# Decoder megakernel on one core: values ahead of keys, router steps moved between slots, masks added strip by strip

## The reference, cut to what matters

```python
# layer 0: keys and values from ctx, queries from x, keys masked; then a dense feed-forward part
scores = jnp.where(mask == 0, -1e20, einsum('bqhd,bkhd->bhqk', q, k))
x = layernorm(softmax(scores / sqrt(256)) @ v @ w_out + b_out + query, g1, beta1)
x = layernorm(relu(x @ w_ff1 + b_ff1) @ w_ff2 + b_ff2 + x, g2, beta2)
# layer 1: cross attention with ctx, residual, layernorm
# layer 2: self attention with a causal mask
scores = jnp.where(tril(ones(S, S)), scores, -inf)
# layer 3: cross attention with ctx, then the experts
router_weights = softmax(x @ rw + rb); topw, topi = top_k(router_weights, 2)
out = sum of the two chosen experts' gelu feed-forward outputs, weighted by softmax(topw)
# layer 4: attention with ctx, one key and value head, keys within 64 of the query; gate, RMS norm
keep = (j >= i - 64) & (j < i + 65)
scores = jnp.where(keep, scores, -1e9)
```

## Time and profile before

| what | value |
|---|---|
| median of 3 runs | 2574.62 us (2570.72 to 2575.63) |
| the profiled execution: its time, its span | 2572.03 us, 2570.2 us |
| busy, share of the span: PE, DVE, ACT, POOL | 90%, 59%, 42%, 37% |
| mean granted clock of TensorE | 0.975 of full speed |

### The profile page before, as it was taken

How to read it: one execution, slowest core, us unless ns; L and a number is a source line. 1 busy time by engine, 2 the same in 40 slices (tenths; PEclk the granted TensorE clock), 3 DMA queues, 4 the chain that set the end, 5 groups by cost and what they waited for, 6 DMA issues and landing times. The chain is left out here.

```text
span 2570.2 us, 78594 instructions
## 1 busy us (share of the span) xinstructions
PE 2325.6 (90%) x29652; PEld 1900.8 (74%) x29653; DVE 1525.4 (59%) x3344; ACT 1079.6 (42%) x2772; POOL 944.7 (37%) x1190
## 2 busy tenths in 40 slices
PE   6999899899899899899898994999999997999997
PEld 4867767767767767767766864999999994666665
DVE  4676676676677677677676676111111114888885
ACT  2344334334334334334334342555555552444443
POOL 3434354344344354354344353200000004556662
PEclk9999999999999999999999997999999997999998
DMA  9201001001001001000000002511111111111110
GB/s 214 95 2 35 2 18 31 6 18 31 5 19 31 6 19 31 6 18 31 6 18 19 2 19 88 173 37 37 35 36 37 37 33 52 50 55 51 51 55 19
DMA packets 89114, 98.12 MB, mean 38 GB/s; under 512 B 23808, under 2 KB 80288, under 8 KB 88736
## 3 DMA queue, kind: packets, MB, share of 16 engines
q1 hardware_dynamic: 79040, 67.20, 8.7%
q0 software_dynamic: 9440, 27.29, 3.4%
q10 hardware_dynamic: 384, 0.01, 0.0%
HBM read 62.21 MB, written 32.24 MB: 37 GB/s over the span
## 5 line engine op out<-in xcount | busy, mean ns | idle before, releaser
L1365 DVE TENSOR_REDUCE mb<-ps_scores 128x8 bf16<-128x1024 f32 x320 | 377.5, 1220 | 107.9 <-PE ps_scores L767 107.8
L1727 POOL TENSOR_TENSOR qbd_all<-qT,consts 128x512 fp32r<-128x512 f32 x160 | 166.4, 1040 | 662.4 <-ACT kT L1112 264.0
L1374 DVE RECIPROCAL rs<-ps_o 128x256 f32<-128x256 f32 x160 | 280.8, 1755 | 43.8 <-PE ps_o L822 41.5
L1126 ACT ACTIVATE pt_all<-ps_scores 128x512 f32<-128x512 f32 x512 | 264.1, 604 | 71.6 <-PE ps_scores L795 71.6
L974 PEld LDWEIGHTS ps_scores<-tiles,w_now 128*128 128x128 f32 x2272 | 266.3, 193 | 5.7 <-ACT w_now L1197 1.3
L974 PE MATMUL ps_scores<-tiles,w_now 128*128 128x128 f32 x2272 | 266.9, 276 | 1.5 <-ACT w_now L1197 0.9
L984 PE MATMUL ps_w<-arena,tiles 128*128 x1136 | 257.1, 379 | 2.5 <-ACT tiles L1205 2.5
L1205 ACT ACTIVATE tiles<-ps_scores,b1s 128x128 f32<-128x128 f32 x568 | 154.1, 382 | 233.6 <-PE ps_w L984 231.2
L1833 POOL DMA_INDIRECT arena<-sorted_y,pidx x64 | 65.9, 1029 | 493.8 <-ACT pidx L1231 478.6
L984 PEld LDWEIGHTS ps_w<-arena,tiles 128*128 128x128 f32 x1136 | 210.4, 190 | 28.5 <-issue 2.9
L1750 POOL TENSOR_TENSOR rstd<-ve,neghalf 128x1 f32<-128x1 f32 x192 | 106.2, 553 | 338.2 <-DVE ve L1385 329.8
(11 more groups left out here) (237 smaller groups left out, 4844.8 us busy)
## 6 DMA issues: line engine op xcount, KB each, us to landing
tiles<-sorted_x SPq DMA_DIRECT2D x72, 128.0 KB, 2.0
sorted_y<-tiles SPq DMA_DIRECT2D x71, 128.0 KB, 1.7
w_experts<-in_L_xattn_e_w SPq DMA_DIRECT2D x6, 1024.0 KB, 12.3
arena<-in_L_xattn_e_w POOLq DMA_DIRECT2D x12, 384.0 KB, 4.1
ct_scratch<-cT SPq DMA_DIRECT2D x32, 128.0 KB, 1.7
x_scratch<-x2b_all SPq DMA_DIRECT2D x32, 128.0 KB, 1.7
arena<-x_scratch SPq DMA_DIRECT2D x32, 128.0 KB, 2.0
cT<-ct_scratch SPq DMA_DIRECT2D x32, 128.0 KB, 2.1
```

What stands on the lines that cost most here:

```text
L1126: nc.scalar.activation(pt[:, 4 * g:4 * g + 4, :].rearrange("p h q -> p (h q)"), ps_s[:, g, :], ACT.Exp, bias=bias, scale=LAYER[l]["scale"] ...
L1365: last = V.tensor_reduce(mb[:].rearrange("p (g r) -> p g r", g=BANKS)[:, 2 * half:2 * half + 2, 0:SLOTS], ps_s[:, 2 * half:2 * half + 2, : ...
L1374: V.reciprocal(rs[:], ps_o[:, 2:4, :]).then_inc(recip_ready, 1)
L1727: G.tensor_tensor(qbd[p].bitcast(F32R), qT[:].unsqueeze(2).to_broadcast([P, KC, PAIR, P]), hmask.unsqueeze(1).unsqueeze(3).to_broadcast([P ...
```

## The change: what it does

It does six things. (1) In light slots `project` makes values, then keys and queries, and waits for `mt_sb` only behind the values; in FF slots and in stage C (argument `keys_first`) layers 1, 3 and 4 make the keys first, as before. (2) Masks are added by strips of 32 rows: the causal and the window mask are stored as four blocks repeated in every strip, and each bank takes four matmuls of 32 rows and 128 columns in place of one of 128 rows and 512 columns; the key mask takes one matmul of 32 rows and 512 columns for each bank. (3) In slots 3 to 6 `router_pieces` stands last on VectorE, behind `qk_lo` and `relu_b`. (4) `rank`, `ranks`, `router_weights` and `positions` move from slot 7 to slot 6, where `rank` stands between `av` and `scores_t`, the scatters from slots 8 to 11 to 7 to 10; the tail of stage A is a slot shorter. (5) In slot 6 `scores_t(now)` stands ahead of `xt(nxt)`. (6) The masks are loaded later: 512 KB for the causal one behind layer 1's weights (waited for and converted on VectorE in slot 3 of iteration 0), 256 KB for the window between stages B and C, in place of 128 KB at the start. The key mask's row is loaded into all 128 partitions, and GpSimd's `mask_row` works on all of them.

```diff
@@ constants()
-    c[:, C_CAUSAL:C_WIN] = np.where(j <= i, 0.0, NEG)
-    c[:, C_WIN:C_ALL] = np.where((j >= i - WINDOW_HALF) & (j < i + WINDOW_HALF + 1), 0.0, NEG)
+    causal = np.where(j <= i, 0.0, NEG)
+    window = np.where((j >= i - WINDOW_HALF) & (j < i + WINDOW_HALF + 1), 0.0, NEG)
+    for at_, m in ((C_CAUSAL, causal.T), (C_CAUSAL + BANKS * P, causal), (C_WIN, window)):
+        blocks = m.reshape(BANKS, ROWS, P).transpose(1, 0, 2).reshape(ROWS, BANKS * P)
+        c[:, at_:at_ + BANKS * P] = np.tile(blocks, (BANKS, 1))
@@ SyncE
-        sp.dma_start(pt[:, 0:2, :], a["consts"][:, C_CAUSAL:C_ALL].rearrange("p (a b) -> p a b", a=2)).then_inc(ld_const, 16)
-            sp.dma_start(kmi[st][0:1, :], a["mask"][bass.ds(b, 1)]).then_inc(mask_loaded[st], 16)
+            sp.dma_start(kmi[st], a["mask"][bass.ds(b, 1)].rearrange("o k -> (o k)").partition_broadcast(P)).then_inc(mask_loaded[st], 16)
+                sp.dma_start(causal_f, a["consts"][:, C_CAUSAL:C_WIN]).then_inc(ld_causal, 16)
...
+        sp.wait_ge(b_down, TILES)
+        sp.dma_start(win_f, a["consts"][:, C_WIN:C_ALL]).then_inc(ld_window, 16)
@@ TensorE: project(n, first_l, keys_first)
-            wait(pe, mt_sb, t)
...
-            if l in (1, 3, 4):
+            keys_first = keys_first and l in (1, 3, 4)
+            if keys_first:
+                wait(pe, mt_sb, t)
                 keys()
             wait(pe, xt_sb, t + 1)
...
             last.then_inc(v_psum, 1)
+            wait(pe, mt_sb, t)
...
-                if l == 2:
+                if not keys_first:
                     keys()
@@
-        def masked(n, g, w, x_):
-            mm(ps_s[:, g, :].rearrange("p (h k) -> p h k", h=SLOTS), w, x_.unsqueeze(1).to_broadcast([P, SLOTS, P]),
-               start=True, stop=False)
+        def masked(blocks, strips):
+            for k in range(BANKS):
+                for g in strips:
+                    at_strip = slice(ROWS * g, ROWS * (g + 1))
+                    mm(ps_s[:, g, :].rearrange("p (h b k) -> p h b k", h=SLOTS, b=BANKS)[:, :, k, :], blocks[at_strip, k, :],
+                       ident_b[at_strip, ROWS * g:ROWS * (g + 1)].unsqueeze(1).to_broadcast([ROWS, SLOTS, ROWS]),
+                       start=k == 0, stop=False, tile_position=(ROWS * g, 0))
+        def keys_masked(n, strips):
+            for g in strips:
+                at_strip = slice(ROWS * g, ROWS * (g + 1))
+                mm(ps_s[:, g, :].rearrange("p (h k) -> p h k", h=SLOTS), ecol_b[at_strip, 0:1].to_broadcast([ROWS, P]),
+                   kmask[n["s"]][at_strip, :].unsqueeze(1).to_broadcast([ROWS, SLOTS, P]), start=True, stop=False,
+                   tile_position=(ROWS * g, 0))
@@ TensorE: run
-            ranked = routed(at_, 8)
+            ranked = routed(at_, 7)
...
-            if ranked:
+            if ranked and not ff_behind:
                 rank(ranked, ff["t"] if ff["ok"] else NT - 1)
...
                 av(prev)
+                if ranked:
+                    wait(pe, ffln_step, 5 * (rk_["j"] * NS + rk_["s"]) + 1)
+                    rank(ranked, ff["t"])
                 if ff["l"] == 0:
                     fxt(ff, 2)
-                    scores_t(now)
+                scores_t(now)
                 xt(nxt)
-                if ff["l"] != 0:
-                    scores_t(now)
-                project(nxt, first and nxt["s"] == 0)
+                project(nxt, first and nxt["s"] == 0, True)
@@ VectorE: run
+            if first and tau == 3:
+                dve.wait_ge(ld_causal, 16)
+                V.tensor_copy(causal_b.rearrange("p a b k -> p (a b k)"), causal_f).then_inc(causal_ready, 1)
...
-            if ranked:
+            if ranked and not (rk_["ok"] and rk_["l"] == 0):
                 ranks(ranked)
...
                 normalise(prev)
+                if ranked:
+                    ranks(ranked)
                 vz_evac(nxt)
-                router_pieces()
                 residual_sum()
                 qk_lo(nxt)
...
-                router_pieces()
             if ff["ok"] and ff["l"] == 0:
                 relu_b(ff)
+            router_pieces()
@@ VectorE, ahead of stage C
+        dve.wait_ge(ld_window, 16)
+        V.tensor_copy(win_b.rearrange("p b k -> p (b k)"), win_f).then_inc(window_ready, 1)
@@ GpSimd
-            G.tensor_scalar(kmask[n["s"]][0:1, :], kmi[n["s"]][0:1, :], 0.0, NEG, ALU.is_equal, ALU.mult).then_inc(kmask_ready, 1)
+            G.tensor_scalar(kmask[n["s"]], kmi[n["s"]], 0.0, NEG, ALU.is_equal, ALU.mult).then_inc(kmask_ready, 1)
...
-                if routed(at_, 9 + s):
-                    scatter(routed(at_, 9 + s), s)
+                if routed(at_, 8 + s):
+                    scatter(routed(at_, 8 + s), s)
```

More of the change, by code:

```diff
@@ L395, in program @@
         dict(scale=0.25, mask=None, bq=None, bk=None, bv=None),
-        dict(scale=0.25, mask=causal_b, bq="L2_xattn_sa_bq", bk="L2_xattn_sa_bk", bv="L2_xattn_sa_bv"),
+        dict(scale=0.25, mask="causal", bq="L2_xattn_sa_bq", bk="L2_xattn_sa_bk", bv="L2_xattn_sa_bv"),
         dict(scale=0.25, mask=None, bq="L2_xattn_ca_bq", bk="L2_xattn_ca_bk", bv="L2_xattn_ca_bv"),
-        dict(scale=0.25, mask=win_b, bq="L3_xattn_bq", bk=None, bv=None),
+        dict(scale=0.25, mask="window", bq="L3_xattn_bq", bk=None, bv=None),
     ]
@@ L752, in scores @@
                 wait(pe, kmask_ready, n["j"] * NS + n["s"] + 1)
+            if l == 2 and n.get("first_l"):
+                pe.wait_ge(causal_ready, 1)
             for half in range(2):
@@ L755, in scores @@
                 strips = range(2 * half, 2 * half + 2)
-                for g in strips:
-                    if mask == "keys":
-                        masked(n, g, one_b[:].to_broadcast([P, P]), kmask[n["s"]])
-                    elif mask is not None:
-                        masked(n, g, ident_b[:], mask[:])
+                if mask == "keys":
+                    keys_masked(n, strips)
+                elif mask is not None:
+                    masked(win_b if mask == "window" else causal_b[:, 0], strips)
                 for u in range(SLOTS):
@@ L779, in scores_t @@
             if not plain:
-                for g in range(BANKS):
-                    masked(n, g, mask[:], ident_b[:])
+                masked(win_b if mask == "window" else causal_b[:, 1], range(BANKS))
             first = plain
@@ L910, in run @@
             if first and tau == 0:
-                pe.wait_ge(ld_const, 32)
+                pe.wait_ge(ld_const, 16)
                 pe.wait_ge(consts_ready, 1)
                 xt(now)
-                project(now, True)
+                project(now, True, False)
+            now["first_l"] = first and now["s"] == 0
             if now["ok"]:
@@ L944, in run @@
                 if nxt["ok"]:
-                    project(nxt, first and nxt["s"] == 0 and nxt["l"] > 0)
+                    project(nxt, first and nxt["s"] == 0 and nxt["l"] > 0, False)
                 if now["ok"]:
@@ L1049, in run_c @@
                 pe.wait_ge(b_y, TILES)
+                pe.wait_ge(window_ready, 1)
                 xt(now)
[L1051 removed]
+                project(now, False, True)
             if now["ok"]:
@@ L1303, in _ @@
             V.memset(vz[i][:], 0.0)
-        for s in range(NS):
-            V.memset(kmask[s], 0.0)
         V.memset(onz[:, 0, 1, :], 0.0)
```

28 lines of the change are left out of this document (15 added, 13 removed).

## The result

The changed kernel takes 2477.04 us (median of 4 runs, 2471.51 to 2478.32) against 2572.67 us for the kernel before in the same comparison: a ratio of 0.9623, 95% interval 0.9604 to 0.9642. The profiled execution took 2476.19 us. The forecast was 2456, the range 2428 to 2500: the direction and the range held, and about 20 us of the expected gain did not come.

What follows compares the result with a forecast made beforehand. TensorE, busy 90% of the span, was taken as the bound, with VectorE nearly the bound in stage C. Terms of 46 + 38 + 16 + 16 = 116 us off 2572.0 gave 2456, range 2428 to 2500.

Steps and rivals of the forecast that it cites:

- Part 1: Light slots of stage A: values fill TensorE's wait for the copied maxima, 0.48 us a slot, 46 us (34 to 54).
- nothing late comes next: Light slots: queries still end the projection and everything behind the values moves up together, so 0.48 us a slot counts.
- Part 2: Stage A: masks by strips shorten TensorE's score matmuls, 4.8 us an iteration, 38 us in all (20 to 51).
- The masks are hardly cheaper: Rival, chance 0.12: new mask matmuls in stages A and C cost twice as much, giving 25 us in place of 54: 2485.
- Part 4: Stage A routing, 7 iterations: moved router steps gain 10.0 us, pay back 5.8 and 2.5; 16 us (-5 to 33).
- the two readings: Router's pieces at their new place on VectorE: 3.4 us by one profile reading, 2.7 by the rule with GpSimd idle.
- the slow clock eats the gain: Rival, chance 0.20: waits in slots 5, 6 and 7 bring 1.2 GHz stretches costing 4.2 us an iteration, not 2.5: 2472.
- Part 3: Stage C: masks by strips save 0.5 us in each of 32 slots, 16 us (9 to 19).
- The step that failed: Stage C: VectorE's waits of 0.28 and 0.25 us can give 0.53; 0.5 taken for each of 32 slots.
- what would show it: Signs: stage C slots of 11.9 to 12.0 us expected; one still above 12.3 would be wrong.
- Costed at nothing: Later mask loads, broadcast key mask, causal conversion on VectorE (once, about 1 us) and moved scatters: no cost counted.

Runs made afterwards that it cites:

- e1: The kernel before with only values made ahead of the wait for the copied maxima in light slots, masks and routing as before; ratio to before 0.9749.
- e2: The changed kernel with the routing move undone: router's pieces ahead of residual sum and `qk_lo`, rank and scatters one slot later; ratio to the kernel before 0.9710.
- e4: The changed kernel with stage C's expansion of the query remainders moved from GpSimd to ScalarE; ratio to the kernel before 0.9551, again 0.9501 (2448.23 us).
- e3: The changed kernel with stage C's window mask added as before, by matmuls of 128 rows and 512 columns; ratio to the kernel before 0.9648.
- e6: The changed kernel with the window masks of stage C (layer 4) left out; ratio to the kernel before 0.9635.
- e10: e9 with rank behind the product with the values in slot 9, ranks behind the reciprocal, weights in slot 8; 2425.80 us, ratio to the kernel before 0.9421.
- e8: The changed kernel with the router's pieces in smaller portions in slots 4 to 7, ranks, weights and positions in slot 8; ratio to the kernel before 0.9675.
- e7: The changed kernel with stage C's window mask as before and the query remainders expanded on ScalarE instead of GpSimd; ratio to the kernel before 0.9655.
- e9: The changed kernel with e4's move and e8's portions, but rank, ranks, weights and positions in slot 9; ratio to the kernel before 0.9494.

## Why the prediction was right, and where it was wrong

**Part 1 (46 us).** Right: 50 by e1, worked out from its iteration 0. The step that said nothing late comes next held; the gain was 0.52 a slot where 0.48 was taken.

**Part 2 (38 us).** Near, but less well shown: 35 by difference (106 less e1's 50 and e2's 21), from groups of both kinds, while e2 against e1, in one slower group, gives 8. By single stretches the masks' cost was read rightly. The second scores gave 0.75 (0.6 taken), the second half of the first 0.32 (0.3), slot 3 gave 0.63 (16.04 to 15.41 in iteration 0; 0.9 taken), slot 0 0.9 (8.9 in e1, 8.0 after; 0.1 taken), slot 1 0.1 (9.19 to 9.08). What the part left out is slot 2: 13.55 in e1, as much after where the clock stays up, and 15.1 to 15.2 in four of six iterations, some 6 us lost in all. *The masks are hardly cheaper* is out.

**Part 4 (16 us).** Right in sum, 21 by e2. By slots, before against after, slot 4 gained 1.6, slot 5 lost 0.2, slot 6 lost 1.6, slots 7 and 8 gained 5.0, of which 2.4 come in iteration 0 too and are not the routing's: 2.4 together, near the 2.3 forecast. The pieces took 3.1 us in the new place (441.89 to 445.01), between the 3.4 and the 2.7 of the two readings; two of them still last 0.45 and 0.51 in place of 0.19. Iterations 1 to 7 have 10 slow stretches, where the kernel before has 14. Six of the ten are in slot 7, behind the longest wait (2.44 us), four in slot 2, away from the router's steps, and none follow the waits of 1.05 and 1.69. So behind the late maxima there are 0.9 an iteration where 1.8 were taken, and *the slow clock eats the gain* did not happen.

**Part 3 (16 us).** Wrong, and it is the whole miss: -6 in place of +16. The step that failed is "VectorE's two waits (0.28 and 0.25) leave it 0.53 us to give. I take 0.5 for each of 32 slots". The waits did go (0.69 to 0.11 a slot), but the step took VectorE's busy time as fixed. It rose by 0.66 a slot (11.03 to 11.68) and took all of it. By the slots (12.79, above the 12.3 of "what would show it") the text's own criterion says wrong. The cause is shown by e4 (take GpSimd's operation away: -0.84), e3 (give TensorE its work back: -0.27) and e6 (take TensorE's work away: nothing). The rival that TensorE's slow stretches did it is out as well: in the second execution of the changed kernel there are fewer (granted clock 0.98 over the 20 middle slots in place of 0.97), its slots are longer (12.92), and so is VectorE's busy time (11.96); and VectorE waits for TensorE only 0.11 us a slot.

The piece of evidence was there: the forecast used the longer pieces beside GpSimd in part 4 and did not ask the same of stage C, where a VectorE operation of 1013 ns stood beside others of the same shape at 425. The Trainium skill (GPSIMD Engine Reference, section Specifications) says that the SBUF interfaces are shared, with contention for VectorE's instructions with two SBUF inputs or in a two-port mode. The rows agree: `yb`, with its inputs in SBUF, more than doubled, while L1375, of whose two inputs one is in PSUM (`ps_qk`), takes 0.34 to 0.35 us beside GpSimd's other expansion (L1757, 20 of 40 in the middle slots) and away from it.

**Costed at nothing.** The first maxima come at 26.7 us in place of 25.0; TensorE waits 10.7 us for the first projection's weights in place of 9.3. With the same loads they came at 25.3 in the second execution of the changed kernel, and at 24.7 to 27.0 in the others, so this is the spread of the start. The 3.2 us between the stages are within such a spread too (588.8 to 600.6 in all runs).

**Numbers.** 100 + 16 was forecast, 106 - 6 came, and some 4 were lost in the spread of start and transition (96 in all by the spans); the range held because it took in a stage C without a gain, not because it had foreseen a loss.

## What to carry to other kernels

Before a saving on one engine is counted, compare the next engine's busy share in that stage, and ask of its busy time too whether it stays: in stage C the same VectorE instructions, at other times against GpSimd's, took 0.66 us more in a slot of 12.5. Look for one shape with two durations in the grouped view; it shows what a shift can cost and what moving the neighbour's operation is worth (here 23 to 29 us). The router's long chain of small steps cost 22 us less (e10 against e4) once it was cut into portions near the slack of each slot and its matmuls stood in the middle of other matmul work; the portions alone (e8) gained nothing.

## What was not expected of the hardware

**A pause of TensorE beside GpSimd's indirect transfers, in some groups of runs.** In the two slower groups slots 8 to 11 take, in the runs with the changed kernel's routing (e3 to e7), 10.4, 11.0, 11.0 and 10.8 us in iterations 1 to 6 in place of 9.0 to 9.2, and 9.23 in iteration 0, which has no indirect stores. TensorE and GpSimd in one such slot of e4:

```profile
505.04 1.30 PE L847 MATMUL ps_o<-pt_all,onz 128*32 128x128 f32 x23
506.65 0.45 PE L847 MATMUL ps_o<-pt_all,onz 128*32 128x128 f32 x5 [0.32 <-issue]
507.38 0.43 PE L847 MATMUL ps_o<-pt_all,onz 128*32 128x128 f32 x4 [0.28 <-issue]
...
504.67 1.05 POOL L1803 DMA_INDIRECT sorted_x<-x2b_all,posu  x1 [0.17 <-issue]
506.03 0.97 POOL L1803 DMA_INDIRECT sorted_x<-x2b_all,posu  x1 [0.30 <-issue]
```

The 32 matmuls take 2.7 us in place of 1.0. Four slots in seven iterations make most of the 49 us between e4's two runs. What TensorE lacks there, and whether the chip or something else of these groups brings it, was not tried.

**The slow clock without a wait.** In e9 the granted clock fell to 0.50 behind rank (0.53 over the window shown), when TensorE had been busy without a gap for 1.9 us; with the same ten narrow matmuls behind 64 others (e10) it stayed at 1.00 in all seven iterations. The Trainium skill (TensorE: Matmul & The Clock Gate, section on HAM oscillation) speaks of waits between bursts; these rows show a fall without a wait right ahead of it; the wait of 0.33 us further ahead stands in e10 as well. What decides stays open: e10 moved ranks and weights as well.
